# VectorE's order in a fused adaLN block: independent instructions between those that wait for each other

## The reference

```
h = layernorm(x) * (1 + ca) + sa
q, k, v = h @ Wqkv.T + bqkv                     # 16 heads of 8
q = (elu(q) + 1.0001) / sqrt(8);  k = elu(k) + 1.0001
num = q . cumsum(k v^T);  den = q . cumsum(k) + 1e-4     # causal linear attention
x = x + ga * layernorm(num / den @ Wout.T + bout) * gamma + beta   # ga over the whole attention output
h = layernorm(x) * (1 + cb) + sb
y = h + softmax_attention(layernorm(h)) @ w_proj         # 16 heads of 8, within a sample
y = y + expert_mlp(layernorm(y))                         # 1 of 8 experts for each token
x = x + gb * y
```

## Time and profile before

| | us |
|---|---|
| median of three runs | 708.53 (706.98 to 710.29) |
| profiled execution: span from its first to its last instruction | 704.9 |
| median less that span, what lies around it | 3.6 |
| VectorE busy | 609.2, 86% of the span |
| TensorE busy | 625.9, 89% |
| ScalarE busy | 495.1, 70% |
| GpSimd busy | 415.7, 59% |

### The profile page before, as it was taken

One profiled execution on the slowest core, in us unless ns is written; L12 is line 12 of the kernel. 1 busy time (PEld: TensorE's weight loads), 2 busy tenths in 40 slices (PEclk: granted clock), 3 DMA queues, 4 the chain that ended last, 5 costly groups with the idle time before them and its releaser, 6 DMA issues.

```text
span 704.9 us, 16370 instructions
## 1 busy us (share of the span) xinstructions
PE 625.9 (89%) x5304; PEld 313.5 (44%) x5304; DVE 609.2 (86%) x1566; ACT 495.1 (70%) x1007; POOL 415.7 (59%) x929
## 2 busy tenths in 40 slices
PE   4588888989876798899999999999999999899994
PEld 2365556656544322222323323233333332498994
DVE  6878999998967998899999999999999995686552
ACT  3644666766645347888888888888898889855662
POOL 4212657565656457135676787887777872566553
PEclk9899989889989859999999999999999999999997
DMA  6563134243362212016420120302103000456500
GB/s 181 182 216 122 61 92 131 95 136 105 121 192 80 89 50 107 26 54 202 122 91 2 58 68 13 113 25 87 39 20 107 24 13 35 139 171 180 168 31 12
DMA packets 42899, 66.25 MB, mean 94 GB/s; under 512 B 7948, under 2 KB 36335, under 8 KB 39808
## 3 DMA queue, kind: packets, MB, share of 16 engines
q1 hardware_dynamic: 39232, 56.73, 26.3%
q0 software_dynamic: 3296, 8.41, 3.3%
q10 hardware_dynamic: 288, 0.07, 0.0%
HBM read 41.64 MB, written 22.26 MB: 91 GB/s over the span
## 4 chain that ended last, share of the span: by engine, by line
PE 48%; DVE 25%; ACT 15%; issue 6%; POOL 3%; SPq 1%; DMA 1%; ACTq 0%; POOLq 0%; DVEq 0%
DVE arena L1561 11%; PE bank L1076 10%; ACT arena L1991 8%; PE pair L1065 6%; PE bank L1037 5%; PE pair L1323 4%; DVE arena L1394 4%; DVE arena L1423 2%; PE pair L1332 2%; PE bank L1332 2%; ACT arena L1960 2%; PE bank L922 2%; PE bank L1087 2%; PE bank L932 1%; PE bank L908 1%
## 5 line engine op out<-in xcount | busy, mean ns | idle before, releaser
L1991 ACT ACTIVATE arena<-pair 128x512 f32<-128x512 f32 x506 | 278.1, 603 | 50.7 <-PE pair L1065 48.8
L1561 DVE TENSOR_REDUCE arena<-bank 128x1 f32<-128x512 f32 x388 | 251.7, 683 | 7.6 <-PE bank L1037 6.5
L1065 PE MATMUL pair<-q_stack,k_stack 64*128 64x512 bf16 x506 | 158.3, 386 | 5.9 <-ACT arena L1991 5.3
L1037 PE MATMUL bank<-k_stack,q_stack 63*128 63x512 bf16 x388 | 138.0, 397 | 8.5 <-DVE arena L1561 4.7
L1076 PE MATMUL bank<-arena,values 128*9 128x512 f32 x1024 | 134.7, 598 | 1.6 <-ACT arena L1991 1.5
L1394 DVE TENSOR_TENSOR arena<-bank,cst 128x512 f32<-128x512 f32 x128 | 82.2, 683 | 16.7 <-PE bank L908 16.6
L1561 DVE TENSOR_REDUCE arena<-pair 128x1 f32<-128x512 f32 x124 | 84.5, 681 | 1.6 <-PE pair L1037 1.2
L715 POOL TENSOR_TENSOR arena<-arena 128x32 f32<-128x32 f32 (+6 forms) x312 | 68.8, 221 | 24.4
L1037 PEld LDWEIGHTS bank<-k_stack,q_stack 63*128 63x128 bf16 x388 | 33.3, 93 | 109.8 <-DVE arena L1561 25.0
L1065 PEld LDWEIGHTS pair<-q_stack,k_stack 64*128 64x128 bf16 x506 | 40.6, 93 | 48.5 <-ACT arena L1991 26.3
L1037 PE MATMUL pair<-k_stack,q_stack 63*128 63x512 bf16 x124 | 49.0, 395 | 0.5 <-ACT v_all L2016 0.3
(11 more groups left out here) (300 smaller groups left out, 1245.1 us busy)
## 6 DMA issues: line engine op xcount, KB each, us to landing
softmax_parts<-arena SPq DMA_DIRECT2D x8, 768.0 KB, 4.1
q_stack<-softmax_parts SPq DMA_DIRECT2D x48, 128.0 KB, 2.9
k_stack<-softmax_parts SPq DMA_DIRECT2D x48, 128.0 KB, 2.9
linear_parts<-arena SPq DMA_DIRECT2D x7, 768.0 KB, 3.7
q_stack<-linear_parts SPq DMA_DIRECT2D x42, 128.0 KB, 2.8
k_stack<-linear_parts SPq DMA_DIRECT2D x42, 128.0 KB, 2.9
arena<-in_L_ffn_w_dram SPq DMA_DIRECT2D x16, 256.0 KB, 4.6
v_all<-token_rows SPq DMA_DIRECT2D x20, 192.5 KB, 2.6
```

Source lines behind the costliest of these rows:

```text
L1037: pe.matmul(bank[:], qs[b % 2][rows, slot, qt * P:(qt + 1) * P], ks[b % 2][rows, slot, :], start=True, stop=True).then_inc(d_s_m, 1)
L1065: pe.matmul(score_bank(s)[:], ks[u][rows, 2 * g + x, kt * P:(kt + 1) * P], qs[u][rows, 2 * g + x, :], start=True, stop=True).then_inc(d_s_ ...
L1561: dve.reduce_max(mx[:, m % 2, col:col + 1], bank[:], AX).then_inc(d_s_mr, 1)
L1991: act.activation(pt[:, kt % 2, x, half, :], score_bank(s)[:], ACT.Exp, scale=SCALE).then_inc(d_s_e, 1)
```

## The change

`stats` is cut in two, `sums` (the four `bn_stats`) and `variances` (the rest), and `normalise` in two, `denominators` (the reciprocal) and `normalise` (the product); `d_normalise` likewise. Nothing is computed otherwise, and only DVE's order changes:

- linear attention, odd slots: reciprocal, `output` of the chunk before, product (it was reciprocal, product, `output`)
- slot 3: reciprocal, `bn_stats` of h, product, `variances` of h, `output`
- slot 0: `bn_stats` of x, then `c_rest`, then `variances` (`c_rest` was first)
- slot 2: `bn_stats` of the input sample ahead of `masked`, `variances` behind it
- slot 4: `bn_stats` of the attention's output ahead of `a_relu`, `variances` behind it
- softmax attention, n = 4 to 29: the product stands behind the first maximum of kt = 2
- the last four chunks: four reciprocals, then four products

```diff
-                def normalise(q):
+                def denominators(q):
                     dve.wait_ge(s_tr, q + 1)
                     heads = b_tr[:].rearrange("p (h w) -> p h w", h=H)
                     dve.reciprocal(den[:, q % 2, :], heads[:, :, E]).then_inc(s_rc, 1)
+
+                def normalise(q):
+                    heads = b_tr[:].rearrange("p (h w) -> p h w", h=H)
                     dve.wait_ge(s_rc, q + 1)
...
-                def stats(src, b, st, mv, ve, s_st, s_mv, s_ve, s_nb):
+                def sums(src, b, st, s_st):
                     for c in range(C):
                         dve.bn_stats(st[:, c, :], tile(src, b, c)).then_inc(s_st, 1)
+
+                def variances(b, st, mv, ve, s_st, s_mv, s_ve, s_nb):
                     dve.wait_ge(s_st, C * (b + 1))
                     wait(dve, s_nb, b)
                     dve.memset(k.spare[:, 0:1], 0.0)
...
                 for s in STEPS:
                     for d in range(NL):
                         g = s * NL + d
+                        if d == 2 and has(s + 3):
+                            a_sums(s + 3)
                         if unit(g) and g:
                             masked(g)
                         if d % 2 == 1 and chunk((g - 3) // 2):
+                            denominators((g - 3) // 2)
+                        if d == 3 and has(s - 2):
+                            c_sums(s - 2, 2)
+                        elif d % 2 == 1 and chunk((g - 5) // 2):
+                            output((g - 5) // 2)
+                        if d % 2 == 1 and chunk((g - 3) // 2):
                             normalise((g - 3) // 2)
-                        if d % 2 == 1 and chunk((g - 5) // 2):
-                            output((g - 5) // 2)
+                        if d == 3 and has(s - 2):
+                            c_variances(s - 2, 2)
+                            if chunk((g - 5) // 2):
+                                output((g - 5) // 2)
                         if d == 0:
+                            if has(s - 2):
+                                c_sums(s - 2, 1)
                             if has(s - 3):
                                 c_rest(s - 3, 0)
                             if has(s - 2):
-                                c_stats(s - 2, 1)
+                                c_variances(s - 2, 1)
                         if d == 1 and has(s - 3):
                             c_rest(s - 3, 1)
                         if d == 2:
                             if has(s + 3):
-                                a_stats(s + 3)
+                                a_variances(s + 3)
...
-                        if d == 3 and has(s - 2):
-                            c_stats(s - 2, 2)
                         if d == 4:
+                            if has(s - 1):
+                                c_sums(s - 1, 0)
                             if has(s + 2):
                                 a_relu(s + 2, 0)
                             if has(s - 1):
-                                c_stats(s - 1, 0)
+                                c_variances(s - 1, 0)
...
                                 maximum(n + 2, 4 * kt + j, ring_bank(n, kt, j))
+                                if j == 0 and kt == 2 and n >= G:
+                                    d_normalise(n - G, ring_bank(n, 1, 4))
...
                         if kt == 1 and n >= G:
-                            d_normalise(n - G, ring_bank(n, kt, 4))
+                            d_denominators(n - G, ring_bank(n, kt, 4))
+                            if n + 2 >= NB:
+                                d_normalise(n - G, ring_bank(n, kt, 4))
...
                 end_stats(0)
+                for f in range(NB - G, NB):
+                    d_denominators(f, ring[f % C])
                 for f in range(NB - G, NB):
                     d_normalise(f, ring[f % C])
```

More of the change, by code:

```diff
@@ L1515, in output_weights, with a_sums, a_variances, c_sums @@
                     assert step[0] == SETUP
-                def a_stats(a):
+                def a_sums(a):
                     dve.wait_ge(w_s_x[min(a, 2)], 16 if a < 2 else 16 * 3)
-                    stats(k.x_all, a, a_st, a_mv, a_ve[:], a_s_st, a_s_mv, a_s_ve, a_s_nb)
-                def c_stats(b, m):
+                    sums(k.x_all, a, a_st, a_s_st)
+                def a_variances(a):
+                    variances(a, a_st, a_mv, a_ve[:], a_s_st, a_s_mv, a_s_ve, a_s_nb)
+                def c_sums(b, m):
                     if m == 0:
@@ L1527, in c_stats, with c_variances @@
                         dve.wait_ge(c_s_h, b + 1)
-                    stats((k.v_all, k.x_all, k.h_all)[m], b, c_st[:, m], c_mv[:, m], c_ve[:, m, :],
-                          c_s_st[m], c_s_mv[m], c_s_ve[m], c_s_nb[m])
+                    sums((k.v_all, k.x_all, k.h_all)[m], b, c_st[:, m], c_s_st[m])
+                def c_variances(b, m):
+                    variances(b, c_st[:, m], c_mv[:, m], c_ve[:, m, :], c_s_st[m], c_s_mv[m], c_s_ve[m], c_s_nb[m])
+                def c_stats(b, m):
+                    c_sums(b, m)
+                    c_variances(b, m)
                 def a_relu(a, z):
@@ L1561, in maximum, with d_denominators @@
                     dve.reduce_max(mx[:, m % 2, col:col + 1], bank[:], AX).then_inc(d_s_mr, 1)
-                def d_normalise(f, bank):
+                def d_denominators(f, bank):
                     heads = bank[:].rearrange("p (h w) -> p h w", h=H)
@@ L1566, in d_normalise @@
                     dve.reciprocal(d_den[:, f % C, :], heads[:, :, E]).then_inc(d_s_fr, 1)
+                def d_normalise(f, bank):
+                    heads = bank[:].rearrange("p (h w) -> p h w", h=H)
                     dve.wait_ge(d_s_fr, f + 1)
```

## The result

Median 696.50 us (696.02 to 697.49, 4 runs) beside 709.33 (706.98 to 710.29, 4 runs) for the kernel before: ratio 0.986, 95% interval 0.9814 to 0.9907. It is 1.4% faster. The direction was forecast, but the gain is 12.8 us by the medians (12.0 against the 708.53 that the prediction started from) where 4.7 had been worked out; the time lies outside the range of 699.5 to 707.6. The profiled execution took 696.64 us with a span of 694.9, 10.0 less than before. That is less than 12.8 because the profiled execution of the kernel before was a fast one: in every run on record the time lies 1.7 to 1.9 us above the span, so it took about 706.7, less than any of its four runs here. (Of the 3.6 us that the prediction took to lie around the span, half is this difference.) What follows explains the 10.0.

A forecast was written before the change was run, and what follows sets the result against it. A step of linear attention was bound by DVE's work up to slot 4's layer norm, then POOL, ACT and PE. Terms 0.8+2.24+0.7+0.6+0.2+0.2 gave 4.7 us, taking 708.53 to 703.8; range 699.5 to 707.6.

The forecast's parts named there:

- what bounds a step of linear attention: Linear attention: DVE's work up to slot 4's layer norm, then POOL, ACT and PE; DVE savings behind it mostly become idle.
- the clock: Linear attention, rival: PE's granted clock falls better, at most 1.0 us a step, 2.0 for two; 0.22 shared with other rivals.
- the hold: Slot 2, steps 3 and 4: POOL's L672 delays DVE's epsilon; rival that DVE slips ahead gains 1.1 us, within a shared 0.22.
- DVE arriving earlier is held until POOL's instruction ends.: Slot 2, steps 3 and 4: earlier savings hardly count, leaving 0.39 us a step, 0.8 for two.
- The size of a broken wait: On DVE: an independent instruction starts 0.17 us after a reciprocal instead of 0.29, saving 0.12, bounds 0 and 0.29.
- the 0.09 for slot 4's layer norm: Slot 4 of linear attention: splitting `bn_stats` from the aggregation saves 0.09 us, bounds 0 and 0.12.
- a broken wait is worth nothing: Rival for the whole kernel: only idle time ahead of `a_relu` is filled, 1.1 us gained, 707.4; chance 0.26, absorbed savings included.
- `a_relu` in slot 4: Steps 1, 2 and 5: `bn_stats` fill DVE's idle time ahead of `a_relu`, gaining 0.85, 0.61 and 0.78, sum 2.24 us.
- Softmax attention: 26 units: 0.02 us lost in each of 21 without a choice, 0.12 gained in each of five with one; net 0.2 gained.
- the last four chunks: Kernel's end: products come some 0.25 us later, but PE's projection waits for ACT, so 0.
- the slower rival: Softmax attention: the normalising product behind a maximum holds PE, 0.3 us a unit, 7.8 in all, giving 712; chance 0.06.
- `output` behind slot 3's layer norm: Linear attention, slot 3: `output` ends about 1.2 us later, `turn_back` up to 0.4 late but covered, cost 0.

The follow-up runs named there:

- Experiment 8: Kernel before with three extra 128x256 products on PE ahead of the turn in slot 6 of steps 1 to 7: 703.23 us, ratio 0.9942.
- Experiment 1: Kernel before with only the change's edits of softmax attention and the last four chunks: 708.93 us, ratio 1.0023.
- experiment 9: Changed linear attention, the rest as before, `a_rest` moved from slot 6 to slot 7 in steps 1 to 5: 710.34 us beside 723.17, ratio 0.9825.
- experiment 3: Kernel before with slot 4's edit alone, `bn_stats` of the attention's output ahead of `a_relu`: 702.70 us, ratio 0.9927.
- experiment 7: Kernel before with only the input sample's epsilon moved from slot 2 to behind slot 3's `masked`: 703.08 us, ratio 0.9926.
- experiment 2: Changed kernel with softmax attention and the last four chunks put back as before: 697.10 us, ratio 0.9851.
- experiment 6: Changed kernel without slot 2's edit, the input sample's `bn_stats` back behind `masked`: 696.94 us, ratio 0.986.
- experiment 5: Changed kernel without slot 4's edit, `a_relu` again ahead of the `bn_stats`: 701.40 us, ratio 0.9918.
- Experiment 4: Kernel before with the order reciprocal, `output`, product in odd slots alone: 703.24 us, ratio 0.993.
- experiment 11: Kernel before with slot 4's new order and the odd slots' order reciprocal, `output`, product, nothing else: 714.97 us beside 723.17, ratio 0.9894.
- experiment 10: Kernel before with slot 4's new order and the input sample's epsilon moved behind slot 3's `masked`: 717.22 us beside 723.17, ratio 0.9913.

## Why the prediction was wrong

The step that failed is the reading of what bounds a step of linear attention; the clock and the hold, both set at nothing, followed from it. The parts in order of what they cost.

**Which limit a step has.** The prediction read a step as DVE's work up to slot 4's layer norm, then a wait chain through POOL, ACT and PE, with slack for DVE behind it. That slack, 0.99 us, was not a second chain of fixed length: it was there only where PE ran at the lower clock for long. Experiment 8 shows it: DVE's order untouched, PE at 1.00, and 1.1 us of step 4 are gone with the idle time. Experiment 1 shows it without any edit to the stage. Over steps 3 and 4 of all traces but experiment 9's, DVE idles 0.95 to 1.04 us behind each step whose clock is 0.87 (four of them) and behind no step at 0.93 or 1.00; experiments 3 and 7 lose the idle time in this way too. Without the idle time a step is nearly DVE's busy time (24.16 of 24.41, 25.66 of 26.06, 25.72 of 26.16), and then everything taken from DVE counts, also what the prediction had called idle time in steps 2 to 4. For step 4 the pieces are: idle time and clock 1.1 (27.27 to 26.16 in experiment 8), the hold and the breaks 1.75 (26.16 to 24.41). By the timelines the 1.75 is the hold's 1.00, three odd slots with 0.19 each, slot 3 with 0.27, slots 0 and 2 with 0.13 each and slot 4 with 0.05, less 0.19 that `state_masked` takes longer behind the short epsilon and 0.15 of `a_rest` in slot 7: 1.81. There is an end to this: experiment 9 takes DVE's busy time to 23.44, and the step stays at 24.36, bound by the chain through ACT and PE.

**The clock, taken as net zero.** It was not. Over steps 2 to 6 the granted clock before is 0.86 to 0.93, after 0.91 and four times 1.00, and steps 1 and 7 lose only 0.12 and 0.07. It is no luck of one trace: over the whole span the granted clock was 0.956 to 0.968 in all twelve runs of the change and of experiments 2 and 6, and 0.942 to 0.956 in the 38 runs of the kernel before. Step 6 holds the most: 3.3 gained, of which 2.7 (25.06 to 22.38) come to the old order too when the clock is up (experiments 7 and 8). In experiment 8 the stage ends 4.6 us earlier than in the kernel before, and in the kernel after 5.8 earlier than in experiment 8. The prediction saw this as a rival and capped a win at 1.0 a step and at steps 3 and 4. The 1.57 us that it read for a step with less of the lower clock (27.27 and 25.70) are not the clock's: step 5 has less work for DVE (23.73 busy, not 25.81), and takes 25.68 in experiment 8 at 1.00. What keeps the clock up in the kernel after is not isolated: PE idles 1.31 us ahead of its turn, hardly less than the 1.51 before, yet it stays at full speed. Where a low stretch falls is not set by the code alone: in experiment 1 linear attention has the old order and step 6 took 23.88 where it took 25.06, and experiment 5's steps 3 and 4 differ by 1.0 with the same code. Step 7's loss of 0.9 stays open: the clock alone does not give it, as experiment 6 has 24.09 there at 0.86.

**"DVE arriving earlier is held until POOL's instruction ends."** It is held only if it arrives second. Before, epsilon starts 0.14 behind L672 (139.73 and 139.59); after, 0.18 ahead. The shortest lead in any trace is 0.04 (experiments 4 and 11), and epsilon lasts 0.17; in step 2 of experiment 9 it starts 0.01 behind and is held for the whole of POOL's instruction:

```profile
87.05 1.27 POOL L672 TENSOR_TENSOR h_all<-arena 128x512 f32<-128x512 f32 x1
...
87.06 1.28 DVE L1435 TENSOR_SCALAR arena<-arena 128x4 f32<-128x4 f32 x1
```

The prediction named that case and took it for the less likely one. Slot 2's row agrees with what the Trainium skill says of the shared port pair ("SBUF — State Buffer"): 1.17 beside POOL's instruction, 0.17 without. Experiment 4 shows that the odd slots' order alone is enough, 6 that slot 2's own part is not needed, 10 the worth of 0.7 us of hold: 0.73 of a step.

**The size of a broken wait.** 0.12 was taken, with 0.17 to the next instruction; the next came after 0.16, but `output` also lasts 0.23 there and not 0.28, and its follower starts after 0.15: 0.19 for the three. Of the 0.09 for slot 4's layer norm, 0.05 came (2.05 us from the pair's start to `masked` before, 145.94 to 147.99; 2.00 after, 140.51 to 142.51). Slot 3's reciprocal and layer norm together gave 0.27 for 0.21 (2.08 and 1.81). In slots 0 and 2 a broken layer norm gave 0.13 each (1.99 to 1.86 and 2.51 to 2.38). So the rival "a broken wait is worth nothing" falls, and with it, for this pair of instructions, the rule of "The DRAIN you can't avoid" in the Trainium skill's "VectorE: DVE Perf Modes", by which only the number of instructions would matter: DVE's instructions are the same 1566, and it is busy for 600.7 us where it was busy for 609.2. The same section also says that a next instruction that is not held starts earlier, which the prediction did not weigh; the 0.16 behind a reciprocal of 0.25 agrees with that.

**`a_relu` in slot 4.** The mechanism was right: no idle time ahead of it in steps 1 to 5. Step 1 lost its 0.85 again, and 0.7 more, to PE at a clock of 0.81: DVE waits 2.11 us for PE's products at 58.48 and 1.23 at 66.97, where it had waited 0.89 (57.09) and 0.76 (64.95). Experiment 2 has the same order with its clock up, and there step 1 is 0.9 shorter than before (22.94 and 23.85), for 1.1 forecast. Experiment 5, which leaves this part out, is 4.5 us above experiment 6, which leaves slot 2's out (701.40 and 696.94). In steps 3 and 4 the prediction gave it 0.09, as DVE came just in time for the exponentials; with the hold gone DVE comes 0.76 too early (experiment 5), and slot 4's order turns that into a gain. Neither part gives the whole: step 4 is 26.06 with slot 4's order, 25.43 with the odd slots', 24.53 with both (experiments 3, 4, 11).

**Softmax attention: 0.6 lost where 0.2 was to be gained.** Units without a choice lose 0.05 and not 0.02, the term that was mis-sized: the maximum comes 0.46 behind its product on PE and not 0.42, so 0.34 after the reciprocal. Units with a choice gained nothing of the 0.12 each, though the maximum starts there as forecast. From the first normalisation's reciprocal to the last 1.24 are lost (266.89 and 268.13 us); the 80 us ahead of them, where nothing of this part lies, are 0.71 shorter.

**Right as worked out:** slot 2's part cost nothing (experiment 6), the last four chunks 0, steps 0 and 5 within about 0.2, and the slower rival did not come. `output` behind slot 3's layer norm held no `turn_back` in steps 0 to 5; in steps 6 and 7 it did, for 0.91 us each, and what that cost is not isolated. The direction was right for reasons that hold, the broken waits and slot 4's order, but they are the smaller part of the gain. By an estimate from experiment 8 (4.6) and two holds of about 0.8, the clock and the hold make some 6 of the stage's 10.5 us, and the prediction had kept both out of its sum.

## What to carry to other kernels

When two engines' paths through a loop are within a few per cent of each other, a gain must be worked out for the loop as a whole: take each engine's busy time per step as a floor, list the idle times on the fullest engine, and ask of each whether the change lets it vanish. Idle time of the fullest engine that stands behind another engine at a lower clock is not slack. Where an instruction of 0.2 us sits in front of a neighbour's 1.3 us one on a shared port, write down the distance between the two: a shift of 0.3 us decides about 1 us.

## What the runs showed of the hardware

An independent instruction behind a 128x16 reciprocal started 0.16 us after its start, a dependent one 0.28 to 0.29; a 128x128 addition in that place lasted 0.23 and not 0.28. The four transposes took 0.66 us at full clock and 1.12 in the stretches at half of it, after waits of 1.31 and 1.51 us; a wait of 1.50 to 1.51 was followed by 0.65 to 0.66 in experiments 3, 7 and 10, with the lower clock behind the transposes, and by 1.11 in experiment 5. An addition of 128x4 on DVE took 0.17 us when it started 0.04 to 0.18 ahead of GpSimd's 1.28 us instruction, and lasted until that one's end when it started 0.01 to 0.59 behind. On one of three chips the kernel before took 723.17 us where it took 708, and in the kernels profiled there the stretch behind softmax attention took 133 us for 118, at a clock of 0.92; linear attention of experiment 9 ended at 223.9 as in the kernel after.
